# The covariance of a whitening kernel: one 128-column product per row, or one 64-column product for each sample group in its own half of TensorE

## The chip, the cores and the metric

The kernel runs on one core of a Trainium2 chip. The metric is the device time of one execution in microseconds (us); the numbers below are of a single program on a single core, so no other core waits for it.

## What is computed

The input `x` is 4 images of 64 channels, 256 by 256, in float32. There are two layers.

```
# layer 0: a long convolution of every channel with a separable filter hx * hy (zero-padded FFT of size 512)
y   = irfft2(rfft2(x) * rfft2(k) / fft_size)[..., :256, :256] + x * bias
# layer 1: whitening over channels, from every 9th position of every channel
x1   = transpose(y, (1, 0, 2, 3)).reshape(64, -1)
x1_s = x1[:, ::9]
cov  = x1_s @ x1_s.T / x1_s.shape[1] + 0.01 * eye(64)
deconv = newton_schulz_inverse_sqrt(cov, 5 iterations)
out  = deconv @ (x1 - mean(x1_s))
```

The kernel does the convolution as products with Toeplitz matrices, and the change touches only how `x1_s @ x1_s.T` and the sums for the mean are formed.

## The kernel before, in words

**Convolution.** 128 units (`UNITS`): two sweeps of 64 channels, two images (`PER`) in a unit. For each unit `q`, `make_v` and `make_y` each issue four groups of matmuls: three in the rounded type fp32r with 256 moving columns (lines 666 to 668) and one in float32 with 128 moving columns (line 669). A float32 matmul of the program is two LDWEIGHTS and two MATMUL instructions in the profile, so 58 of them are 116 instructions of each kind; an fp32r one is a single pair. ScalarE rounds `x` and `v` (L434, L443) and flips the filters (L424, L425), VectorE subtracts (L523, L532) and finishes `y` with the bias (`finish_y`, L543), GpSimd multiplies `y` by a 0/1 mask that keeps every ninth position (L400), and VectorE sums each group of nine columns into `z_sb` (`sum_masked`, L551): one of the nine is a sample, the others are zero.

**z_sb.** It has `ZROWS` = 58 rows `r`. A row holds, for each of the 128 partitions, 129 float32 columns (`ZW`): 64 channels of sample group j = 0, 64 channels of sample group j = 1, and one column of ones. A sweep fills it once.

**Covariance.** For each of the 58 rows one float32 matmul takes the 128 channel columns as stationary and all 129 as moving, and accumulates 128 x 129 results. Of these only the two diagonal 64 x 64 blocks and the column of sums are used; the two off-diagonal blocks mix group 0 with group 1 and are thrown away. It is done twice: for sweep 0 inside the unit loop at `q == C + 2` = 66, into PSUM bank 2, and copied to `sums_first` (L564); for sweep 1 after the loop, into bank 0, on top of `sums_first`, which a matmul with the identity puts there first (line 726). The two blocks are then copied to `sums`, the upper one by ScalarE (L463), the lower one by VectorE (L603, L604), and added by a matmul with `twice` (line 739).

**After it.** Five Newton-Schulz steps (lines 746 to 761) with `keep_busy` matmuls (L717) between them give `dmat`; then 64 tiles of 1 MB (`TILES`) are multiplied by it (line 777), shifted by the mean on ScalarE (L475) and VectorE (L646), and stored. The first sweep's and second sweep's `y` went to DRAM (`convolved`), so tiles are loaded again. 14 tiles (`KEPT`) are loaded during the second sweep, 12 more around its end (L314), each as its room in SBUF comes free: the last four of these wait for `cov_mm`, 2, since they land on `z_sb`. Then in the transform the loads follow the stores. All DMAs are issued by SyncE's queue in program order.

**What orders the work.** Every engine's order is written out by hand, and semaphores join them. TensorE runs `make_v(q + 1)`, `make_y(q)`, and at `q == 66` the covariance, then `make_y(66)`, `make_v(67)`. The covariance waits for `z_done`; VectorE waits for `cov_mm` before it copies and goes on.

Of the kernel before, what the change touches and what calls it, by code (L numbers as in the profile page):

```python
# [13 lines left out]
P = 128  # L14
B, C, S = 4, 64, 256
# [30 lines left out]
ZROWS = BLOCKS * GROUPS // 2  # L46
ZW = 2 * C + 1
# [19 lines left out]
def conv_whiten(nc, x, first, hidden, columns, bias, out):  # L67
# [3 lines left out]
    with ExitStack() as ctx:  # L71
        def sb(name, shape, dt=F32):
            return ctx.enter_context(nc.sbuf_tensor(name, shape, dt))
# [40 lines left out]
        z_sb = z_all[:, :].rearrange("p (r m) -> p r m", m=ZW)  # L114
# [3 lines left out]
        mask = sb("mask", [P, MASK_COLS])  # L118
        bias_sb = sb("bias_sb", [P, C])
        ident = sb("ident", [P, P])  # L120
        sums, sums_first = sb("sums", [P, C + 1]), sb("sums_first", [P, ZW])
        small = sb("small", [P, 8])
        col = sb("col", [P, 4])
        chan_i, chan, rate = sb("chan_i", [P, 1], I32), sb("chan", [P, 1]), sb("rate", [P, 1])
# [23 lines left out]
        for t in range(TILES):  # L148
# [3 lines left out]
            k = in_at[t]  # L152
# [14 lines left out]
        ps = ctx.enter_context(nc.psum_tensor("ps", [P, 8, S * 2], F32))  # L167
# [39 lines left out]
            return x_sb[slot].rearrange("p (b h w) -> p b h w", b=PER, h=HB)[:, :, h, :]  # L207

        def z_of(c):
            return z_sb[:, :, 0:2 * C].rearrange("p r (j c) -> p r j c", j=2)[:, :, :, c]  # L210

        def grouped(k, lo, hi):
            return masked[k][:, lo:hi, :].rearrange("p i w -> p (i w)").rearrange("p (r j u) -> p r j u", j=2, u=STRIDE)
# [136 lines left out]
        @block.gpsimd  # L350
        def _(pool):
            n_step = [0]

            def chained(ins):

                n_step[0] += 1
                ins.then_inc(pool_step, 1)
                pool.wait_ge(pool_step, n_step[0])

            def split_x(q):  # L360
                if q >= UNITS:
                    return
                k = q % 2

                wait(pool, x_hi_done, q + 1)
                nc.gpsimd.tensor_tensor(x_lo[k], row_block(q % X_SLOTS, 0), x_hi[k].bitcast(F32),  # L366
                                        ALU.subtract).then_inc(x_lo_done, 1)

            nc.gpsimd.memset(w_sb, 0.0).then_inc(w_zeroed, 1)
            nc.gpsimd.iota(pos_i, pattern=[[-1, S]], base=S - 1, channel_multiplier=0)  # L370
            chained(nc.gpsimd.iota(chan_i[:], pattern=[[0, 1]], base=0, channel_multiplier=1))
            nc.gpsimd.tensor_copy(pos, pos_i)
            nc.gpsimd.tensor_copy(chan[:], chan_i[:]).then_inc(pos_ready, 1)
            nc.gpsimd.memset(filt, 0.0).then_inc(filt_zeroed, 1)
            nc.gpsimd.memset(small[:], 0.0).then_inc(filt_zeroed, 1)
            nc.gpsimd.iota(index.bitcast(I32), pattern=[[1, MASK_COLS]], base=0,
                           channel_multiplier=S % STRIDE).then_inc(index_ready, 1)
            split_x(0)

            for k in range(2):  # L380
                nc.gpsimd.memset(masked[k][:, :, S:], 0.0)
            chained(nc.gpsimd.memset(ident[:], 0.0))
            chained(nc.gpsimd.affine_select(out=ident[:], in_=ident[:], compare_op=ALU.not_equal, fill=1.0,
                                            base=0, pattern=[[-1, P]], channel_multiplier=1))
            chained(nc.gpsimd.memset(z_sb[:, :, 2 * C:], 1.0))
            split_x(1)

            def mask_y(q):
                if q < 0:
                    return  # L390
                k = q % 2
                wait(pool, y_done, q + 1)

                wait(pool, z_done, q - 1)
                if q == LAST - 1:
                    for b in range(PER):
                        nc.gpsimd.tensor_tensor(masked_of(k, b, 1), by_image(y_sb[k])[:, b:b + 1],
                                                mask_of(SWEEPS - 1, b, 1), ALU.mult).then_inc(masked_half, 1)
                    return
                nc.gpsimd.tensor_tensor(masked_of(k, 0, PER), by_image(y_sb[k]), mask_of(q // C, 0, PER),  # L400
                                        ALU.mult).then_inc(masked_done, 1)

            for q in range(UNITS):
                split_x(q + 2)
                mask_y(q - 1)


            nc.gpsimd.tensor_scalar(ident15, ident[:], 1.5, None, ALU.mult)
            chained(nc.gpsimd.tensor_scalar(ident_eps, ident[:], EPS, None, ALU.mult))
            for k in range(2):  # L410
                nc.gpsimd.tensor_tensor(twice[:, k * C:(k + 1) * C], ident[:, 0:C], ident[:, C:P], ALU.add)
            pool.wait_ge(z_last_done, 2 * PER)
            nc.gpsimd.memset(halves, 0.5).then_inc(ident_ready, 1)

        @block.scalar
        def _(act):
            def flip(q):
                if q >= UNITS:
                    return
                k, h = q % T_SLOTS, q % H_SLOTS  # L420
                act.wait_ge(hankel_loaded[h], 32 * (q // H_SLOTS + 1))

                wait(act, y_mm, q - T_SLOTS + 1)
                nc.scalar.copy(t_f32[k], hankel[h][:, :, :P - 1:-1])  # L424
                nc.scalar.copy(t_hi[k], hankel[h][:, :, ::-1]).then_inc(flipped, 1)  # L425

            def round_x(q):
                if q >= UNITS:
                    return
                k = q % X_SLOTS  # L430
                act.wait_ge(x_loaded[k], 16 * (q // X_SLOTS + 1))

                wait(act, v_mm, q - 1)
                nc.scalar.copy(x_hi[q % 2], row_block(k, 0)).then_inc(x_hi_done, 1)  # L434

            def round_v(q):
                k = q % 2
                wait(act, v_mm, q + 1)

                wait(act, y_mm, q - 1)  # L440
                nc.scalar.copy(v_f32[k], ps_v[k][:, :, S:2 * S])  # L441

                nc.scalar.copy(v_hi[k], ps_v[k][:, :, 0:S]).then_inc(v_hi_done, 1)  # L443

            act.wait_ge(rate_ready, 1)
            nc.scalar.activation(decay, pos, ACT.Exp, scale=rate[:]).then_inc(decay_ready, 1)
            round_x(0)
            for layer in range(3):
                act.wait_ge(f_dve, layer + 1)
                nc.scalar.activation(hid, arg, ACT.Sin).then_inc(f_sin, 1)  # L450
            round_x(1)
            flip(0)
            flip(1)

            for q in range(UNITS):
                round_v(q)
                round_x(q + 2)
                flip(q + 2)

            act.wait_ge(filt_zeroed, 2)  # L460
            nc.scalar.activation(small[:, 7:8], small[:, 7:8], ACT.Sqrt)
            act.wait_ge(cov_mm, 2)
            nc.scalar.copy(sums[C:P, :], ps[C:P, 0, C:ZW]).then_inc(sums_upper, 1)  # L463
            act.wait_ge(norm_mm, 1)
            nc.scalar.activation(small[:, 1:2], ps[:, 0, 0:1], ACT.Sqrt).then_inc(n_act, 1)
            act.wait_ge(n_act, 1)
            nc.scalar.activation(small[:, 3:4], small[:, 1:2], ACT.Sqrt).then_inc(n_act, 1)
            act.wait_ge(d_ready, 1)

            for t in range(TILES):  # L470
                act.wait_ge(t_mm[0], t + 1)

                wait(act, t_stored[out_at[t]], 16 * stores_before_out[t])
                src = ps[:, bank(t, 0):bank(t, 0) + 2, :].rearrange("p r n -> p (r n)")
                nc.scalar.activation(places[out_at[t]][:, 0:TW // 2], src, ACT.Identity,  # L475
                                     bias=small[:, 6:7]).then_inc(t_act, 1)

        @block.vector
        def _(dve):
# [77 lines left out]
            for q in range(UNITS):  # L557
                split_v(q)
                finish_y(q - 1)
                split_t(q + 2)  # L560
                if q == C + 2:

                    dve.wait_ge(cov_mm, 1)
                    nc.vector.tensor_copy(sums_first[:], ps[:, 2, 0:ZW]).then_inc(cov_out, 1)  # L564
                if q < LAST:
                    sum_masked(q - 2)

# [32 lines left out]
            sum_half(LAST, 1)  # L600

            dve.wait_ge(cov_mm, 2)
            nc.vector.tensor_copy(sums[0:C, 0:C], ps[0:C, 0, 0:C])  # L603
            nc.vector.tensor_copy(sums[0:C, C:C + 1], ps[0:C, 0, 2 * C:ZW]).then_inc(sums_ready, 1)  # L604
            chained(nc.vector.memset(cov, 0.0))
            dve.wait_ge(ident_ready, 1)
            dve.wait_ge(cov_mm, 3)
# [42 lines left out]
        def _(pe):  # L650
# [44 lines left out]

            def covariance(bank_of_cov, rows, first):
                for r in rows:
                    last = mm(ps[:, bank_of_cov, 0:ZW], z_sb[:, r, 0:2 * C], z_sb[:, r, :],  # L698
                              start=(r == first), stop=(r == ZROWS - 1))
                return last  # L700

            make_v(0)
# [20 lines left out]


            pe.wait_ge(v_lo_done, LAST)
            mm(ps[:, 0, 0:ZW], ident[:], sums_first[:], start=True, stop=False)
            pe.wait_ge(z_done, LAST - 1)
            for b in range(PER):
                w = ZROWS // PER
# [81 lines left out]
```

## Time and profile before

| | before |
|---|---|
| time, median of 3 runs | 936.75 us (936.08 to 941.52) |
| time of the profiled execution | 937.11 us |
| its span in the trace | 934.9 us |
| granted TensorE clock, mean | 0.995 |
| PE busy | 865.4 us (93%) |
| PEld busy | 729.6 us (78%) |
| DVE busy | 577.7 us (62%) |
| POOL busy | 494.3 us (53%) |
| ACT busy | 401.6 us (43%) |
| DMA | 306.35 MB, mean 328 GB/s |

PE is TensorE's matmuls, PEld its weight loads, which run beside them. Spans are between the first and the last record of the trace; the time of an execution is a little longer (937.11 against 934.9 us). A matmul's duration in the trace is its latency; several are in flight at once, so what one costs in a row of them is the distance from start to start. Where a row has a count, its busy time is the union of their durations.

### The profile page before, as it was taken

The numbers are of one execution on the slowest core, as the hardware profiler recorded it, in microseconds if no ns is written. First come the engines' busy times: TensorE is split into PE (matmuls) and PEld (weight loads), VectorE is DVE, ScalarE is ACT, GpSimd is POOL, SyncE is SP. The second block draws the span as 40 slices with busy tenths as digits, with TensorE's granted clock in tenths as the row PEclk, the third lists the DMA queues.
The fourth block names the chain that finished last, engine by engine and source line by source line (L and its number), as shares of the span: only waits on it lengthen the run. The fifth ranks groups of instructions, "written<-read, shape, count | busy, mean of one in ns | idle before, by whom it ended". The sixth has DMA issues, their size and how long they took to land.

```text
span 934.9 us, 15604 instructions
## 1 busy us (share of the span) xinstructions
PE 865.4 (93%) x5970; PEld 729.6 (78%) x5970; DVE 577.7 (62%) x641; ACT 401.6 (43%) x715; POOL 494.3 (53%) x278
## 2 busy tenths in 40 slices
PE   2699999999999999999999999999999999977773
PEld 0699999999999999999999999999644444432221
DVE  5388888888878856787887787875333333322221
ACT  2355555555555534555555555551133333321220
POOL 2298888888888865787887778873000000000000
PEclk9999999999999999999999999999999999999997
DMA  3799999999989984999999999997999999999998
GB/s 106 242 305 287 282 284 285 283 281 287 288 278 296 285 256 150 348 342 321 358 345 314 323 331 353 344 325 256 407 381 422 423 424 422 426 427 427 427 427 342
DMA packets 99349, 306.35 MB, mean 328 GB/s; under 512 B 13483, under 2 KB 48332, under 8 KB 84684
## 3 DMA queue, kind: packets, MB, share of 16 engines
q1 hardware_dynamic: 99276, 305.37, 91.8%
q8 instruction: 47, 0.77, 0.3%
q14 instruction: 26, 0.21, 0.1%
HBM read 167.96 MB, written 137.36 MB: 327 GB/s over the span
## 4 chain that ended last, share of the span: by engine, by line
PE 83%; DMA 12%; DVE 2%; issue 1%; ACT 1%; SPq 0%; DVEq 0%
PE ps L669 24%; PE ps L777 15%; PE ps L666 13%; PE ps L667 13%; PE ps L668 13%; DMA arena<-convolved 11%; PE ps L698 3%; DVE arena L503 1%; PE ps L717 0%; DMA arena<-filters 0%; ACT arena L475 0%; DVE arena L646 0%; PE ps L657 0%; SPq L317 0%; DMA arena<-hidden 0%
## 5 line engine op out<-in xcount | busy, mean ns | idle before, releaser
L669 PE MATMUL ps<-arena 128*128 128x128 f32 x2048 | 393.8, 274 | 0.0
L666 PE MATMUL ps<-rounded 128*128 128x256 f32 x1024 | 373.7, 365 | 11.5 <-DVE rounded L532 8.7
L400 POOL TENSOR_TENSOR arena<-arena,mask 128x1024 f32<-128x1024 f32 x126 | 325.7, 2585 | 69.1 <-DVE arena L543 68.8
L669 PEld LDWEIGHTS ps<-arena 128*128 128x128 f32 x2048 | 315.9, 190 | 0.0
L668 PE MATMUL ps<-rounded 128*128 128x256 f32 x1024 | 288.8, 282 | 0.0
L667 PE MATMUL ps<-rounded 128*128 128x256 f32 x1024 | 288.2, 281 | 0.0
L777 PE MATMUL ps<-arena 128*128 128x512 f32 x488 | 215.7, 597 | 25.6 <-DMA arena<-convolved 25.6
L543 DVE SCALAR_TENSOR_TENSOR arena<-arena,bias_sb,ps 128x1024 f32<-128x1024 f32 x127 | 162.6, 1280 | 91.3 <-PE ps L669 45.8
L777 PEld LDWEIGHTS ps<-arena 128*128 128x128 f32 x488 | 90.8, 190 | 149.5 <-issue 105.7
L666 PEld LDWEIGHTS ps<-rounded 128*128 128x128 f32 x1024 | 196.8, 192 | 12.7 <-issue 12.7
L366 POOL TENSOR_TENSOR rounded<-arena,rounded 128x512 fp32r<-128x512 f32 x128 | 165.2, 1291 | 77.3 <-ACT rounded L434 76.6
L667 PEld LDWEIGHTS ps<-rounded 128*128 128x128 f32 x1024 | 197.3, 193 | 0.0
L668 PEld LDWEIGHTS ps<-rounded 128*128 128x128 f32 x1024 | 192.9, 188 | 0.0
L646 DVE TENSOR_SCALAR arena<-ps,small 128x1024 f32<-128x1024 f32 x64 | 82.2, 1284 | 170.3 <-PE ps L777 170.3
L551 DVE TENSOR_REDUCE arena<-arena 128x116 f32<-128x1044 f32 x126 | 155.5, 1234 | 0.0
L475 ACT ACTIVATE arena<-ps,small 128x1024 f32<-128x1024 f32 x64 | 71.2, 1113 | 188.5 <-PE ps L777 188.5
L441 ACT COPY arena<-ps 128x512 f32<-128x512 f32 x128 | 75.0, 586 | 171.2 <-PE ps L669 171.1
L523 DVE TENSOR_TENSOR rounded<-ps,rounded 128x512 fp32r<-128x512 f32 x128 | 88.1, 688 | 33.0 <-ACT rounded L443 32.6
L434 ACT CAST rounded<-arena 128x512 fp32r<-128x512 f32 x128 | 80.5, 629 | 45.7 <-DMA arena<-x 45.4
L532 DVE TENSOR_TENSOR rounded<-arena,rounded 128x512 fp32r<-128x512 f32 x128 | 89.7, 701 | 12.5 <-ACT rounded L425 12.4
L424 ACT COPY arena<-arena 128x256 f32<-128x256 f32 x128 | 51.8, 405 | 80.9 <-PE ps L669 67.6
L425 ACT CAST rounded<-arena 128x512 fp32r<-128x512 f32 x128 | 78.9, 617 | 0.0
(93 smaller groups left out, 218.9 us busy)
## 6 DMA issues: line engine op xcount, KB each, us to landing
arena<-x SPq DMA_DIRECT2D x128, 512.0 KB, 5.4
convolved<-arena SPq DMA_DIRECT2D x256, 256.0 KB, 5.3
out<-arena SPq DMA_DIRECT2D x64, 1024.0 KB, 11.8
arena<-convolved SPq DMA_DIRECT2D x47, 1024.0 KB, 17.6
arena<-filters SPq DMA_DIRECT2D x256, 128.0 KB, 4.7
arena<-convolved SPq DMA_DIRECT2D x28, 512.0 KB, 6.0
filters<-arena SPq DMA_DIRECT2D x16, 192.0 KB, 3.5
rounded<-convolved SPq DMA_DIRECT2D x3, 1024.0 KB, 8.8
```

Of the source, the lines that this page charges most:

```text
L366: nc.gpsimd.tensor_tensor(x_lo[k], row_block(q % X_SLOTS, 0), x_hi[k].bitcast(F32), ALU.subtract).then_inc(x_lo_done, 1)
L400: nc.gpsimd.tensor_tensor(masked_of(k, 0, PER), by_image(y_sb[k]), mask_of(q // C, 0, PER), ALU.mult).then_inc(masked_done, 1)
L523: nc.vector.tensor_tensor(v_lo[k], ps_v[k][:, :, 0:S], v_hi[k].bitcast(F32), ALU.subtract).then_inc(v_lo_done, 1)
L532: nc.vector.tensor_tensor(t_lo[k], hankel[h][:, :, ::-1], t_hi[k].bitcast(F32), ALU.subtract).then_inc(t_lo_done, 1)
L543: nc.vector.scalar_tensor_tensor(y_sb[k], x_sb[q % X_SLOTS], bias_sb[:, q % C:q % C + 1], ps_y[k].rearrange("p a n -> p (a n)"), ALU.mult, ...
L551: nc.vector.tensor_reduce(z_of(q % C), grouped(q % 2, 0, BLOCKS), AX_X, ALU.add).then_inc(z_done, 1)
L646: nc.vector.tensor_scalar(places[out_at[t]][:, TW // 2:TW], src, small[:, 6:7], None, ALU.add).then_inc(t_dve, 1)
L666: mm(wide, hi[:, b, cols], t_hi[k][:, f, :], start=True, stop=False)
L667: mm(wide, hi[:, b, cols], t_lo[k][:, f, :], start=False, stop=False)
L668: mm(wide, lo[:, b, cols], t_hi[k][:, f, :], start=False, stop=False)
L669: last = mm(o[:, b, m * S + P:(m + 1) * S], block1[:, b, cols], t_f32[k][:, f, :], start=False, stop=True)
L777: last = mm(ps[:, bank(t, u) + r, :], dmat, places[k][:, w:w + IMG], start=True, stop=True)
```

## The change

The two groups' products are made apart. A row of `z_sb` is laid out anew: group 0, the ones, group 1. For each row there are two matmuls in place of one: group k has 64 stationary columns and 65 moving ones (its channels and the ones), writes 64 PSUM partitions, and has the tile position `(0, 64 * k)`, that is all 128 rows of the array and one half of its columns. For group 1 the ones come first, so its sums stand in column 0 of its half, and the copies to `sums` follow: ScalarE now makes two, VectorE one.

```diff
-        sums, sums_first = sb("sums", [P, C + 1]), sb("sums_first", [P, ZW])
+        sums, sums_first = sb("sums", [P, C + 1]), sb("sums_first", [P, C + 1])
...
         def z_of(c):
-            return z_sb[:, :, 0:2 * C].rearrange("p r (j c) -> p r j c", j=2)[:, :, :, c]
+
+            return z_sb[:, :, c:c + C + 2:C + 1]
...
-            chained(nc.gpsimd.memset(z_sb[:, :, 2 * C:], 1.0))
+            chained(nc.gpsimd.memset(z_sb[:, :, C:C + 1], 1.0))
...
             act.wait_ge(cov_mm, 2)
-            nc.scalar.copy(sums[C:P, :], ps[C:P, 0, C:ZW]).then_inc(sums_upper, 1)
+            nc.scalar.copy(sums[C:P, C:C + 1], ps[C:P, 0, 0:1])
+            nc.scalar.copy(sums[C:P, 0:C], ps[C:P, 0, 1:C + 1]).then_inc(sums_upper, 1)
...
                     dve.wait_ge(cov_mm, 1)
-                    nc.vector.tensor_copy(sums_first[:], ps[:, 2, 0:ZW]).then_inc(cov_out, 1)
+                    nc.vector.tensor_copy(sums_first[:], ps[:, 2, 0:C + 1]).then_inc(cov_out, 1)
...
             dve.wait_ge(cov_mm, 2)
-            nc.vector.tensor_copy(sums[0:C, 0:C], ps[0:C, 0, 0:C])
-            nc.vector.tensor_copy(sums[0:C, C:C + 1], ps[0:C, 0, 2 * C:ZW]).then_inc(sums_ready, 1)
+            nc.vector.tensor_copy(sums[0:C, :], ps[0:C, 0, 0:C + 1]).then_inc(sums_ready, 1)
...
             def covariance(bank_of_cov, rows, first):
                 for r in rows:
-                    last = mm(ps[:, bank_of_cov, 0:ZW], z_sb[:, r, 0:2 * C], z_sb[:, r, :],
-                              start=(r == first), stop=(r == ZROWS - 1))
+
+                    for k in range(2):
+                        lo = k * (C + 1)
+                        last = mm(ps[k * C:(k + 1) * C, bank_of_cov, 0:C + 1], z_sb[:, r, lo:lo + C],
+                                  z_sb[:, r, k * C:(k + 1) * C + 1], start=(r == first), stop=(r == ZROWS - 1),
+                                  tile_position=(0, k * C))
                 return last
...
-            mm(ps[:, 0, 0:ZW], ident[:], sums_first[:], start=True, stop=False)
+            mm(ps[:, 0, 0:C + 1], ident[:], sums_first[:], start=True, stop=False)
```

**Where the instructions stand.** On TensorE between `make_y(65)` and `make_y(66)`, before the change (the size is partitions of the output by its columns, the stationary width being the first):

```order
L666 MATMUL ps<-rounded 128x256
L667 MATMUL ps<-rounded 128x256
L668 MATMUL ps<-rounded 128x256
L669 MATMUL ps<-arena 128x128
L698 MATMUL ps<-arena 128x129 x58
L666 MATMUL ps<-rounded 128x256
```

At the same place with the change, where line 698 has become 702 and 666 to 669 have become 667 to 670:

```order
L667 MATMUL ps<-rounded 128x256
L668 MATMUL ps<-rounded 128x256
L669 MATMUL ps<-rounded 128x256
L670 MATMUL ps<-arena 128x128
L702 MATMUL ps<-arena 64x65 x116
L667 MATMUL ps<-rounded 128x256
```

Nothing moved; 58 matmuls of the program became 116 of half the width. On TensorE at the end of the unit loop, before the change, from the busy-keeping matmuls to the norm of the covariance:

```order
L717 MATMUL ps<-ident 128x128 x9
L726 MATMUL ps<-sums_first,ident 128x129
L698 MATMUL ps<-arena 128x129 x58
L717 MATMUL ps<-ident 128x128 x3
L739 MATMUL ps<-sums,arena 128x65
L717 MATMUL ps<-ident 128x128 x5
L742 MATMUL ps<-small,arena 128x1
```

And with it:

```order
L722 MATMUL ps<-ident 128x128 x9
L731 MATMUL ps<-sums_first,ident 128x65
L702 MATMUL ps<-arena 64x65 x116
L722 MATMUL ps<-ident 128x128 x3
L744 MATMUL ps<-sums,arena 128x65
L722 MATMUL ps<-ident 128x128 x5
L747 MATMUL ps<-small,arena 128x1
```

Here too the order stays, and the matmul with the identity has 65 moving columns in place of 129.

## Rows read from the trace of the kernel before

**Rows 1.** The page: TensorE's clock and the DMA in 40 slices of the span

```profile
PE   2699999999999999999999999999999999977773
...
PEclk9999999999999999999999999999999999999997
DMA  3799999999989984999999999997999999999998
GB/s 106 242 305 287 282 284 285 283 281 287 288 278 296 285 256 150 348 342 321 358 345 314 323 331 353 344 325 256 407 381 422 423 424 422 426 427 427 427 427 342
```

**Rows 2.** Stretches: PE, PEld, DVE, ACT, POOL busy (and count), clock, DMA share, GB/s

```profile
200.00:300.00 100.00, 100.00 (x870) 100.00 (x869) 80.47 (x87) 55.29 (x110) 87.67 (x44) 1.00 0.91 286
340.00:354.00 14.00, 14.00 (x127) 14.00 (x126) 2.41 (x5) 0.93 (x2) 3.56 (x2) 1.00 0.52 168
400.00:500.00 100.00, 100.00 (x865) 100.00 (x864) 78.02 (x86) 54.75 (x109) 78.42 (x44) 1.00 0.99 339
```

**Rows 3.** Chain that ended last, in order of time: start, us, what

```profile
340.51 12.96 PE ps L698 x116
...
644.01 13.19 PE ps L698 x116
657.21 0.67 PE ps L717 x6
...
669.16 134.02 PE ps L777 x312
803.21 1.29 DVE arena L646
804.57 0.33 SPq L317
804.95 23.49 DMA arena<-convolved
```

**Rows 4.** Timeline, around the second covariance's start

```profile
643.98 0.19 PEld L698 LDWEIGHTS ps<-arena 128*128 128x128 f32 x1 [1.28 <-issue]
644.01 0.35 PE L698 MATMUL ps<-arena 128*128 128x129 f32 x1 [1.11 <-DVE arena L581]
```

**Rows 5.** Timeline from 657.80 to 657.90 us: 65 moving columns

```profile
657.60 0.28 PE L717 MATMUL ps<-ident 128*128 128x128 f32 x1
657.71 0.33 PE L739 MATMUL ps<-sums,arena 128*128 128x65 f32 x2
657.72 0.19 PEld L739 LDWEIGHTS ps<-sums,arena 128*128 128x128 f32 x1
657.83 0.19 PEld L717 LDWEIGHTS ps<-ident 128*128 128x128 f32 x1
657.88 0.33 PE L717 MATMUL ps<-ident 128*128 128x128 f32 x1
```

**Rows 6.** Tile `sums`: duration in ns, least/median/most

```profile
L739 PE MATMUL ps<-sums,arena x2: 222/248/275, 657.7 to 657.8; 128*128 128x65 f32 x2
L463 ACT COPY sums<-ps x1: 209/209/209, 657.2 to 657.2; 64x65 f32<-64x65 f32 x1
L604 DVE COPY sums<-ps x1: 141/141/141, 657.4 to 657.4; 64x1 f32<-64x1 f32 x1
```

**Rows 7.** Timeline after the first covariance, in `make_y(66)`

```profile
353.77 0.19 PEld L666 LDWEIGHTS ps<-rounded 128*128 128x128 f32 x1
353.80 0.36 PE L666 MATMUL ps<-rounded 128*128 128x256 f32 x1
```

**Rows 8.** Stretches after the unit loop, columns as in rows 2

```profile
644.00:654.00 10.00, 9.99 (x89) 10.00 (x90) 2.42 (x4) 0.00 (x0) 0.31 (x2) 1.00 1.01 405
654.00:658.00 4.00, 4.00 (x38) 4.00 (x37) 0.42 (x3) 0.21 (x1) 0.00 (x0) 1.00 0.97 315
658.00:676.00 18.00, 17.20 (x88) 11.64 (x88) 7.38 (x26) 2.60 (x4) 0.00 (x0) 1.00 1.02 425
...
676.00:688.00 12.00, 12.00 (x30) 5.30 (x29) 5.14 (x4) 3.34 (x3) 0.00 (x0) 1.00 0.93 339
...
800.00:928.00 128.00, 94.87 (x208) 37.32 (x206) 34.44 (x27) 28.95 (x26) 0.00 (x0) 0.99 1.01 427
```

**Rows 9.** Who waited for whom: total us, times, longest

```profile
PE ps L777 <- DMA arena<-convolved: 25.6, 22, 1.2
```

**Rows 10.** SyncE's queue: the first stores of the transform

```profile
674.17 7.13 SPq L317 DMA_DIRECT2D out<-arena  x3
```

## The prediction

> **What bounds the kernel now.** I read the page's slices first [rows 1]: TensorE is busy in all but the first and the last ten slices, at full clock, and the DMA is near its ceiling (427 GB/s) only in those last ones. So there are two stages. In the unit loop TensorE has no gap over 100 us at a time [rows 2], VectorE and GpSimd are at 80 to 88%, and the DMA at 286 GB/s: time taken off TensorE there comes off the end. In the second stage, the transform of 64 tiles, the stretches show the DMA at 1.01 and 427 GB/s from 800 us on while TensorE is at 95 of 128 us [rows 8], and TensorE waits for loads 22 times, 25.6 us in all [rows 9]: there the bytes set the end. Between them lies the second covariance.
>
> The chain has the two covariances as pieces of 12.96 and 13.19 us, each of 116 MATMUL instructions [rows 3]. The first is wholly TensorE's: in its 14 us VectorE, ScalarE and GpSimd come nearly to rest and the DMA falls to 168 GB/s [rows 2]. During the second the DMA moves 405 GB/s [rows 8]: tiles are loaded beside it.
>
> **The covariance itself.** 58 rows in 13.1 us are 0.226 us a row, two pairs of a load and a matmul of 0.113 us each. What limits a pair? The last small matmul before the norm tells. It has 128 stationary columns and 65 moving ones. Its first instruction starts at 657.71; the two together are busy 0.33 us and the second lasts 275 ns [rows 5, 6], so the second starts at 657.71 + 0.33 - 0.275 = 657.77, 0.06 us later: 65 moving columns cost 59 ns or so, half of what 129 cost. But the loads stand at 657.60, 657.72 and 657.83 [rows 5], 0.11 us apart although the columns stream in half the time: a load of 128 columns takes 0.11 us by itself. So before the change load and stream are equal, and both are halved by it: 59 ns for the stream, and, as an estimate by columns, 56 ns for the load of 64. But there are four pairs a row in place of two. One after the other they make 4 x 59 = 236 ns, a little more than the 226 of before. **All of the gain hangs on whether the two halves of the array work at the same time.**
>
> If they do, the order in the program still limits them: half 0's two instructions come one after the other (59 ns), then half 1's first may start beside half 0's second, then 59 ns, then the next row. A row is 2 x (59 + d), where d is the step from one half to the other. No row shows such a step. The nearest is a switch between types of matmul: the second instruction of line 669 starts about when the load of L666 does, at 353.77, and the matmul of L666 at 353.80 [rows 7], so 0.03 us. So d is between 0 and 28 ns with overlap (and 59 without). I take the middle, 14: a row is 146 ns, a covariance 58 x 0.146 = 8.5 us in place of 13.1, **4.6 us less**. With d = 0 it is 118 ns a row and 6.3 us less, with d = 28 it is 174 ns and 3.0 us less.
>
> Entering and leaving the divided array may need the pipeline empty, twice per covariance. No row shows it; it is bounded by nothing and by one latency of 275 ns each time [rows 6]. I take the whole, 0.5 us for a covariance, since I don't see what would hide it.
>
> The page "TensorEngine Tiling (Array Packing)" of the Trainium skill, section Key Properties, says that different tiles can load and multiply in parallel and that a change of tiling mode drains TensorE; no row here shows either. Another page of the Trainium skill, "TensorE: Matmul & The Clock Gate", section "Back-to-back issue gap", gives about 81 ns per pair of load and matmul at 128 moving columns as the sustained rate; by it four pairs would be 324 ns a row, 5.7 us more in each covariance. It was not measured in float32, and the 59 ns in this trace between two matmuls with 65 columns are below it.
>
> **First covariance.** TensorE is alone on the path, so 4.6 - 0.5 = 4.1 us come off in full. What is behind it is ready: the x slots are full, since the DMA has come down to 168 GB/s beside it [rows 2], and VectorE's copy to `sums_first` has 65 columns rather than 129 and is beside `make_y(66)`. `z_of` writes two groups 65 columns apart rather than 64: the same 116 sums per unit, no cost, hidden by TensorE anyway (VectorE is at 80% [rows 2]).
>
> **Second covariance.** It also ends 4.1 us sooner, and so do `dmat` and the first store. The small edits: ScalarE copies twice; the second one adds about 0.14 us (as L604's 141 ns for a single column [rows 6]), VectorE saves as much, and the `keep_busy` instructions after the covariance (0.67 us [rows 3]) cover both copies. Nothing. What the 4.1 us are worth depends on the DMA, which is the bound soon after. Its rate when full is 425 GB/s [rows 8]. From 654 to 658 it moves 315: 4 x (1 - 315/425) = 1.0 us of transfer lost. I read that as the early loads running out before the four tiles that land on `z_sb` may go (they wait for this covariance). From 676 to 688 it moves 339: 12 x (1 - 339/425) = 2.4 us lost, the 12 first tiles being in and the stores only starting. An earlier covariance fills such holes and nothing else. By bytes they are 3.5 us; by the share of time in which DMA engines rest, 4 x 0.03 + 12 x 0.07 = 1.0 us, the rest being slow packets that would stay slow. The gain here is between 1.0 and 3.5; I take **2.0 us**, nearer to the lower end, since in the stretches of 315 GB/s the share is 0.97. So about half of the second covariance's gain is given back.
>
> **Sum.** 4.1 + 2.0 = 6.1 us. The profiled execution took 937.11 us, so 931.0 by it; it lies 0.36 us over the median of 936.75, and against that the forecast is 930.7. Ends of this case: 6.3 - 0 + 3.5 = 9.8, 927.0; 3.0 - 0.5 + 1.0 = 3.5, 933.3.
>
> **Rivals.**
>
> *No overlap (also: the tile position changes nothing).* The halves take turns, or their loads do. 4 x 59 = 236 ns a row, 58 x 0.010 = 0.6 us more, and 0.5 for the mode: 1.1 us more in each. In the second one the later `dmat` starves the DMA for as long, so 2.2 in all: 938.9; with loads at 56 ns as the limit and no drain it is 936.5. For it: in this trace a load never overlaps another load of the same kind closer than 0.11 us, though durations of 0.19 us overlap, so there is one load path now. Against: nothing, but nothing in the trace speaks for a second path being closed either.
>
> *The load is no longer hidden (slower).* Before, each load runs beside the matmul in front of it. When the array has to be waited for, a matmul starts 31 ns after its load at the earliest: 643.98 and 644.01 [rows 4], 353.77 and 353.80 [rows 7]. If in a divided array every pair shows that much of its load, and the halves don't overlap, a pair is 59 + 31 = 90 ns, a row 360 ns and a covariance 20.9 us, 7.8 more; twice, and 0.5 each for the mode, is 16.6: 953. If the whole load of 56 ns shows, a row is 460 ns and it is 26.7 us, 13.6 more, twice with the mode 28.2: 965. It is slower by over 1% from about 4.7 us per covariance on, 81 ns a row less the 10 of the turns, so from 18 ns shown of each load. It speaks for it that each half is loaded anew while it is in use; against it, that in rows of before the load of the next matmul starts while the last one is in flight, in the same rows and columns of the array [rows 5]. The Trainium skill, "TensorE: Matmul & The Clock Gate", section "The mechanism", names a rule that would bring it about: loads overlap with matmuls in flight only when their row group differs (or when they go to the background buffer), and both halves here use all rows. By the rule's first half alone the load would not have been hidden before either, and the trace shows it hidden.
>
> *The clock.* Each matmul now uses half of the array. The granted clock is 1.00 through both covariances [rows 2, 8] with a full one. If it fell to the lower level in them, pitches would double: from 8.5 us to 17, some 4 us above before in each, 943 to 946. I see no row that speaks for it.
>
> **How the numbers follow.** A measurement of this kernel can tell about 1% (9.4 us) from no change: faster is under 927.4, slower over 946.1. Overlap 0.52 (927 to 933), no overlap 0.27 (936 to 939), load shown 0.16 (up to 945 for small parts of it, 0.03; 953 to 965, 0.13), clock 0.05. The likeliest is overlap, at 930.7. Faster by over 1% needs nearly both best ends at once: 0.07. Slower by over 1%: 0.13 from shown loads and 0.02 from the clock, 0.15. The rest, 0.78, is within. The range of 8 in 10 begins at the best end of the overlap, 927, takes in the turns and small shown loads, and ends at 944; 965 is left out.
>
> **What would show it.** In the changed trace the covariance's group has 464 matmul instructions; the piece of the chain should be 6.8 to 10.1 us long rather than 13. Loads of the two halves at nearly the same start, and matmuls of 64x65 alternately 59 and about 14 ns apart, show overlap; an even 56 to 59 ns shows turns; 90 or more shows the load. The stretch from 340 us on should end 4 us sooner, the first store (674.17 before [rows 10]) by 8 us, the last transfer by only 6, and the hole of 315 GB/s should be smaller. If the first covariance is 4 us shorter and the end moves by 4 alone, the second one's share was mis-sized; if it moves by 8, the DMA was not the bound that I take it for.

## The result, and the profile after

The changed kernel took a median of 930.75 us (926.39 to 934.42, 8 runs) against 939.57 us (936.08 to 941.52, 8 runs) for the kernel before, measured together: ratio 0.9901, 95% interval 0.9877 to 0.9926. That is 9.3 us less (7.0 to 11.6). The forecast was 6.1 us less than 936.75, the median of the three runs shown before; the absolute numbers nearly meet, 930.7 and 930.75, but that is luck: the kernel before came out 2.8 us slower in the larger set. The saving was half as large again as forecast, and the forecast saving lies just outside the measured interval.

The chain of the changed kernel, in order of time (start, us, what), answers to [rows 3]; the span is 927.3 us (934.9 before):

```profile
339.34 6.92 PE ps L702 x232
...
638.13 6.60 PE ps L702 x219
644.74 1.35 issue
646.08 0.57 PE ps L702 x13
646.66 0.86 PE ps L722 x6
...
658.78 127.16 PE ps L782 x296
785.96 1.29 DVE arena L647
787.32 0.33 SPq L318
787.70 23.33 DMA arena<-convolved
```

The first covariance is 6.92 us in place of 12.96, with twice as many instructions. The second is 6.60 + 1.35 + 0.57 = 8.52 us in place of 13.19, with a pause of 1.35 us near its end that the first does not have.

The group of the covariance's instructions, durations in ns (least, median, most), and the timeline around 340.25 us and at the end of the first covariance:

```profile
L702 PEld LDWEIGHTS ps<-arena x464: 132/138/138, 339.3 to 646.4; 128*64 128x64 f32 x155
L702 PE MATMUL ps<-arena x464: 218/222/271, 339.3 to 646.4; 128*64 128x65 f32 x155
```

```profile
340.08 0.46 PE L702 MATMUL ps<-arena 128*64 128x65 f32 x10
...
345.79 0.46 PE L702 MATMUL ps<-arena 128*64 128x65 f32 x10
345.91 0.20 PEld L702 LDWEIGHTS ps<-arena 128*64 128x64 f32 x4
346.18 0.19 PEld L667 LDWEIGHTS ps<-rounded 128*128 128x128 f32 x1
```

Ten matmuls of 0.222 us fill 0.46 us, so the last starts 0.46 - 0.22 = 0.24 us after the first: nine steps of 0.027 us on average, where each alone was to cost 0.059. In the single records the starts of the matmuls come in pairs, 7 ns apart, with a pair every 58 ns, and those of the loads do the same: the two halves run side by side. At the end the last matmul starts at 346.03 (345.79 + 0.46 - 0.22) and the next load at 346.18; that is 0.15 us, some 0.09 more than a step of 0.058.

The stretches, columns as in [rows 2] and [rows 8]:

```profile
340.00:354.00 14.00, 14.00 (x283) 13.93 (x278) 4.52 (x6) 3.26 (x8) 3.62 (x3) 1.00 0.45 136
...
640.00:658.00 18.00, 15.86 (x250) 14.16 (x246) 6.53 (x27) 0.64 (x4) 0.20 (x1) 1.00 1.00 403
658.00:690.00 32.00, 32.00 (x79) 14.41 (x78) 10.94 (x11) 10.03 (x9) 0.00 (x0) 1.00 1.00 395
690.00:800.00 110.00, 109.90 (x256) 48.18 (x254) 40.89 (x32) 35.65 (x32) 0.00 (x0) 1.00 1.01 427
800.00:920.00 120.00, 85.13 (x185) 33.06 (x184) 30.81 (x24) 25.62 (x23) 0.00 (x0) 0.98 1.01 427
```

The clock stays at its full level in both covariances. The first store is issued at 663.79 in place of 674.17 [rows 10], 10.4 us earlier, and the span ends 7.6 us earlier: 2.8 us were given back in the DMA-bound stage. Single spans are to be read with care here: short pauses of TensorE in the second sweep, which the profile gives as "issue" and which come and go from run to run (none in e1_first_only, 7.2 us in sum in e5_second_left_out), move the start of the second covariance by several microseconds whatever the kernel.

### The profile page after: what moved, and what is told of

Same layout as the page of the kernel before. It is cut to its first block, busy times and chain, and to the rows that moved or that the text cites. A ratio compares the mean times of both kernels' runs of the same rounds, so it can differ in the third digit from the quotient of the medians.

```text
span 927.3 us, 16068 instructions
## 1 busy us (share of the span) xinstructions
PE 854.4 (92%) x6202; PEld 717.6 (77%) x6202; DVE 578.9 (62%) x640; ACT 400.7 (43%) x716; POOL 494.4 (53%) x278
## 4 chain that ended last, share of the span: by engine, by line
PE 73%; DMA 17%; DVE 3%; SPq 3%; issue 1%; ACT 1%; DVEq 0%; ACTq 0%
PE ps L670 21%; PE ps L782 15%; PE ps L667 12%; PE ps L668 11%; PE ps L669 11%; DMA arena<-convolved 11%; DMA convolved<-arena 4%; PE ps L702 2%; DMA arena<-x 1%; SPq L262 1%; DVE arena L545 1%; SPq L272 1%; SPq L318 1%; DVE arena L505 1%; PE ps L722 0%
## 5 line engine op out<-in xcount | busy, mean ns | idle before, releaser
L534 DVE TENSOR_TENSOR rounded<-arena,rounded 128x512 fp32r<-128x512 f32 x128 | 91.8, 717 | 11.5 <-ACT rounded L426 11.5
```

The lines of the kernel that those rows point to most:

```text
L534: nc.vector.tensor_tensor(t_lo[k], hankel[h][:, :, ::-1], t_hi[k].bitcast(F32), ALU.subtract).then_inc(t_lo_done, 1)
```

## The experiments

The profiled lengths of the first covariance are compared first (from the chain), then the times. Runs with one time only are read for their traces.

**e3_half_by_half, e4_two_rows, e7_blocks_16, e11_blocks_4: does the order of the halves matter?** The edit is the same in all, with `BLOCK` 58, 2, 16 and 4 (the changed kernel has 1):

```diff
-                for r in rows:
-                    for k in range(2):
+                rows = list(rows)
+                for at in range(0, len(rows), BLOCK):
+                    for k in range(2):
+                        for r in rows[at:at + BLOCK]:
```

> The kernel after, with the same matmuls in another order: in each call of covariance all of half 0's rows, then all of half 1's. Theory A (a matmul starts only after the one before it in the program has, so two halves work together only where they alternate): 232 instructions at 58 ns, 13.5 us for the first covariance, as before the change. Rival B (the gain is from smaller loads and streams and not from working at the same time): the order doesn't matter, 6.9 us.

> As the kernel after, but two rows of half 0, then two rows of half 1, in turn. If matmuls start strictly in the program's order, with a step of nearly nothing from one half to the other, two rows take 2 x (4 - 1) x 58 = 348 ns, a row 174 ns and the first covariance 10.1 us. If TensorE starts a matmul of the free half ahead of one that waits for the busy half, it is 6.9 us again. If the order of the two float32 passes in the machine isn't that of the program (the starts 7 and 51 ns apart in the changed kernel could mean that), it is something between.

> As the order with two rows, but 16 rows of half 0, then 16 rows of half 1 (32 instructions of each kind in a run). Two rows gave full overlap and 58 rows none. If TensorE looks ahead in a window of 64 instructions, loads counted, it sees the other half only in the last part of each run: about half of the overlap, a first covariance of 9 to 12 us. If the window is much smaller it is about 12.5 to 13.5 us, if larger 7.2.

> Four rows of half 0, then four rows of half 1 (runs of 8 matmul instructions). With 16 rows the starts came in pairs for about three instructions around each switch from one half to the other, and the first covariance took 12.5 us: (32 - 3) x 7.25 x 0.058. By the same look-ahead of three instructions, four rows give (8 - 3) x 29 x 0.058 = 8.4 us. If the look-ahead is longer than that it is 7.2 us, as with two rows.

The pieces of the chain of e3_half_by_half, e7_blocks_16 and e11_blocks_4, in this order:

```profile
340.27 13.50 PE ps L703 x232
```

```profile
339.66 12.43 PE ps L703 x232
```

```profile
339.46 8.66 PE ps L703 x229
```

The group of e4_two_rows, in the window of the first covariance:

```profile
L703 PE MATMUL ps<-arena x232: 219/222/271, 339.2 to 346.2; 128*64 128x65 f32 x116
```

In e4_two_rows the first covariance is 7.18 us from the first record to the last (6.99 in the changed kernel, 13.57 in e3_half_by_half, 12.50 in e7_blocks_16, 8.73 in e11_blocks_4). So half by half each step is 13.50 / 232 = 0.058 us, and the whole gain is gone with the same instructions, the same loads and the same streams: **it comes from the two halves working at the same time**, and rival B is out. Theory A, as it was put before the run, is out too: with two rows in a run, strict order of starts would have made 10.1 us, and it was 7.2. TensorE starts matmuls of one half while earlier ones of the other half still wait, but only a few ahead. In the single records of e7_blocks_16 the starts are 58 ns apart within a run, and for about three steps at each change of half they come in pairs. From a look-ahead of three, 8.4 us was expected for four rows in a run, and it was 8.7.

**e8_narrow: what sets the 58 ns?**

```diff
-                    covariance(2, range(ZROWS), 0).then_inc(cov_mm, 1)
+                    covariance(2, range(1), 0)
+                    covariance(2, range(1, ZROWS), 0, 33).then_inc(cov_mm, 1)
```

(The last argument is the number of moving columns. The sums that the missing columns would give are left out, and `covariance` got the argument for it; the lines of that are not shown.)

> The kernel after, but in the first covariance rows 1 to 57 have 33 moving columns in place of 65 (the rest of the sums of sweep 0 is left out); the stationary 64 stay. If the load of 64 columns sets the pitch as well as the stream (56 against 59 ns), the first covariance stays at about 6.6 us. If the load is hidden entirely, it falls to about 3.5 to 4 us.

```profile
341.74 6.89 PE ps L702 x232
```

6.89 us with 33 moving columns and 6.92 with 65: with half of the moving columns a step is no shorter, so the stream is not what holds it at 58 ns. I read it as the load: 64 float32 columns in 58 ns, where 128 take 0.11 us [rows 5]. No run changed the stationary width alone, so a fixed cost of a float32 pair is not ruled out. Halving the moving columns alone would have brought nothing. Both halves load every 58 ns, so their loads, too, run side by side.

**e9_switches: what does it cost to divide and join the array?**

```diff
                                   tile_position=(0, k * C))
+                    if bank_of_cov == 2:
+                        mm(ps[:, 3, 0:1], ident[:], ident[:, 0:1], start=True, stop=True)
```

> The kernel after, but in the first covariance each row's two halves are followed by one float32 matmul of the whole array (128 stationary columns, 1 moving) into a bank that nothing reads: the array is divided and joined 58 times in place of once. The extra matmul's two loads of 128 columns take 2 x 0.11 us, so without a cost of the switch a row is 0.117 + 0.22 = 0.34 us and the first covariance 19.7 us. If each switch empties the pipeline and costs up to one latency of 0.275 us, twice a row, it is up to 0.89 us a row, 52 us. By what the changed trace shows at the end of the covariance (0.15 us from the last matmul's start to the next load) I expect 0.1 us for each switch, 31 us.

The first covariance took 50.65 us, where 31 was expected. Pieces of the chain near its start and near its end, and stretches of it:

```profile
343.71 0.27 PE ps L702 x4
343.97 0.31 PE ps L706 x2
...
390.11 0.41 PE ps L702 x4
390.52 0.52 PE ps L706 x2
```

```profile
344.00:347.00 3.00, 3.00 (x32) 2.58 (x32) 0.00 (x0) 0.00 (x0) 1.27 (x1) 1.00 0.96 282
...
345.00:390.00 45.00, 45.00 (x300) 38.42 (x296) 0.00 (x0) 0.00 (x0) 0.27 (x1) 0.52 0.07 26
```

At full clock a row of six matmuls takes 0.27 + 0.31 = 0.58 us. Without a cost of the switch it would be 0.34, so two switches cost 0.24 us, 0.12 each, close to the 0.1 expected. From 345 to 390 us the granted clock is 0.52, that is the lower level for nearly all of it, and a row takes 0.41 + 0.52 = 0.93 us. Ten rows at 0.58 and 48 at 0.93 make 50 us; all 58 at full clock would be 34. TensorE was never idle by the profile in those 45 us, so the time at the switches is counted as busy there. The changed kernel makes this switch four times in all, which by this price is 0.5 us.

**e1_first_only and e2_second_only: what is each covariance worth?** Both use the layout of before, with a column of ones ahead of row 0, so that group 0 can take the ones of the row ahead; `covariance_halves` is used in one place, the old function in the other (the copies to `sums` and `sums_first` that go with it are not shown).

```diff
+            def covariance_halves(bank_of_cov, rows, first):
+                for r in rows:
+                    for k in range(2):
+                        at = 1 + r * ZW + k * C
+                        last = mm(ps[k * C:(k + 1) * C, bank_of_cov, 0:C + 1], z_all[:, at:at + C],
+                                  z_all[:, at - 1 + k:at + C + k], start=(r == first), stop=(r == ZROWS - 1),
+                                  tile_position=(0, k * C))
+                return last
```

> Only the covariance of sweep 0 (at unit 66) is made by halves; that of sweep 1 keeps the 128-column matmuls of before. To serve both, group 0's ones are read from the column ahead of its row, and VectorE makes three small copies to sums_first. My theory (the first covariance lies on TensorE's path alone, its 6.0 us come off in full): time 6.0 us below before, ratio 0.9936, the first covariance's piece 6.9 us, the second's about 13 us. Rival (what the end gained came from the second one, which released DMAs earlier, and the first one's gain is taken back in the second sweep, where the DMA share is 0.99): less than 2 us below before.

> The mirror: only the covariance of sweep 1, after the unit loop, is made by halves. My theory (the DMA sets the end of the second stage, so an earlier second covariance only fills holes in it): first store 6 us earlier than in before against the end of the unit loop, but the time only 1 to 3 us below before, 2.0 by the prediction's value, ratio 0.998. Rival (the path goes through the covariance and the norm to the end): 6 us below before, ratio 0.9935.

e1_first_only: 935.24 us (12 runs) against 940.59 (23 runs), ratio 0.9942 (0.9918 to 0.9966), 5.5 us less (3.2 to 7.7). Its first covariance took 7.1 us in place of 13.0; these 5.8 us are inside, and the rival's less than 2 us is out. e2_second_only: 937.33 us (12 runs), ratio 0.9955 (0.9926 to 0.9984), 4.2 us less (1.5 to 7.0; the two medians differ by 3.3). The interval holds both the 2.0 of the prediction and the rival's 6; it doesn't decide.

**e5_second_left_out and e12_later_norm: the same question from both sides.** The first leaves out 56 of the 58 rows of the second covariance.

```diff
-                last = covariance(0, range(b * w, (b + 1) * w), -1)
+                last = covariance(0, range((b + 1) * w - 1, (b + 1) * w), -1)
```

> The kernel after, but the covariance of sweep 1 leaves out 56 of its 58 rows (only row 28 and row 57 go in), so the whitening rests on too few samples; everything else is done. The second covariance falls from 6.9 us, 8.5 with its pause, to about 0.3. If the DMA sets the end of the second stage, little is left to gain from it: 0 to 2 us below the kernel after, 0.990 to 0.988 against before. If the covariance is on the path to the end, 6 to 8 us below the kernel after: ratio 0.982 to 0.983.

```diff
-            keep_busy(3)
+            keep_busy(33)
```

> The kernel after, with 33 in place of 3 busy-keeping matmuls between the second covariance and the addition of its halves: 60 instructions of 0.111 us, 6.7 us. The four loads that wait for the second covariance go as early as in the kernel after, but the matrix dmat and the first store come 6.7 us later, as if that covariance were as long as before. If what an earlier second covariance brings comes by way of the first store (holes in the DMA's work after the first loads are in), the time is 2 to 4 us above the kernel after: ratio 0.992 to 0.9945 against before. If it comes by the release of the four loads, or if nothing of it reaches the end, it is that of the kernel after, 0.990; if TensorE's chain sets the end, 6.7 us more: 0.997.

e5_second_left_out: 931.59 us (6 runs), ratio 0.9921 (0.9890 to 0.9951). It is no faster than the changed kernel (0.9901); by the two intervals at most 2 us of gain can hide. The covariance did not shrink to the 0.3 us expected, though. Around it, by the chain:

```profile
646.77 1.22 DVE arena L583 x2
647.99 0.04 issue
648.04 0.48 PE ps L702 x4
648.52 1.58 PE ps L722 x6
```

Its second part waits for the samples that VectorE sums last (L583), so from its first matmul to the end of its last it takes 3.0 us in place of 8.5. And TensorE, idle for 1.67 and 2.16 us before the two parts, then runs at the lower clock for a while, so that the steps to `dmat` take longer:

```profile
648.00:653.00 5.00, 4.96 (x25) 4.85 (x26) 1.54 (x7) 0.35 (x3) 0.20 (x1) 0.50 1.02 421
```

The transform starts 3.9 us earlier than in the changed kernel (the table below), not 8. e12_later_norm: 937.88 us (12 runs), ratio 0.9971 (0.9943 to 0.9998), so 0.0070 above the changed kernel, 6.6 us, with an uncertainty of some 3.5 from the two intervals: delaying `dmat` costs it all or most of 6.7 us, though the four loads go as early. It was above the range of 2 to 4 that my theory gave, and at the rival's value; the traces below put it at 6.6. The hole that the theory asked for is there, though it is not the whole of it. From 658 to 690 us, e12_later_norm:

```profile
658.00:690.00 32.00, 31.84 (x90) 15.45 (x91) 11.41 (x15) 8.92 (x8) 0.00 (x0) 1.00 0.92 365
```

The DMA engines rest for 8% and move 365 GB/s, where the changed kernel has 1.00 and 395.

Since the pauses of the second sweep blur the times, I also took from each trace the length of the second stage alone, which is the time from the first matmul of the second covariance to the end of the span, beside the time from the same matmul to the transform's first one:

| kernel | to the transform, us | to the end, us |
|---|---|---|
| e12_later_norm | 27.4 | 295.8 |
| e3_half_by_half | 26.8 | 295.5 |
| before | 25.0 | 290.9 |
| e1_first_only | 25.0 | 292.1 |
| e7_blocks_16 | 24.5 | 293.4 |
| e11_blocks_4 | 21.4 | 288.3 |
| e2_second_only | 20.9 | 291.8 |
| changed | 20.5 | 289.2 |
| e4_two_rows | 20.5 | 289.1 |
| e8_narrow | 20.4 | 288.4 |
| e9_switches | 20.3 | 287.4 |
| e5_second_left_out | 16.6 | 288.4 |
| e10_bf16_whole | 16.2 | 288.7 |
| e6_bf16 | 15.6 | 290.6 |

The mean of the three around 25 us is 292.1, of the six around 21 us 289.0, of the three around 16 us 289.2; single values scatter by 1 to 2 us, so a difference of two means is uncertain by about 1 us. Going from 25 to 21 us brought 3.1 us at the end, and going on to 16 us nothing: there the DMA sets the end. Above 21 us the end moves with the transform's start. (The transform's start in e3_half_by_half and e5_second_left_out contains a stretch at the lower clock.)

Where do these microseconds lie? The first 270 us of that stage, before, changed and e12_later_norm:

```profile
644.01:914.01 270.00, 244.81 (x695) 116.02 (x696) 88.53 (x94) 69.73 (x66) 0.30 (x2) 1.00 1.01 419
```

```profile
638.13:908.13 270.00, 241.06 (x814) 110.24 (x814) 88.59 (x94) 70.83 (x67) 0.20 (x1) 1.00 1.01 421
```

```profile
634.25:904.25 270.00, 242.35 (x863) 115.13 (x864) 87.14 (x92) 68.71 (x66) 0.30 (x2) 1.00 1.00 415
```

The stage moves about 120 MB in all three. Against 427 GB/s these stretches have lost 5.1, 3.8 and 7.6 us of transfer. So of the 6.6 us by which e12_later_norm is longer than the changed kernel, 3.8 are such holes. The other 2.8 lie in the last 19 to 26 us of the span, where the last stores land, and no run shows why. The means of the groups in these 270 us are 418, 420.5 and 421 GB/s, so holes account for about half of the 3.1 us.

**e6_bf16 and e10_bf16_whole: a version that is faster than both.** The samples are rounded to bfloat16 as VectorE writes them; the rest is as in the changed kernel (e6_bf16) or as in the kernel before (e10_bf16_whole).

```diff
-        z_sb = z_all[:, :].rearrange("p (r m) -> p r m", m=ZW)
+        z_sb = z_all[:, :].bitcast(mybir.dt.bfloat16)[:, 0:ZROWS * ZW].rearrange("p (r m) -> p r m", m=ZW)
```

> The kernel after with the samples z_sb in bfloat16, so each matmul is one pair of instructions and not two, and the samples are rounded (64 stationary, 65 moving columns, still by halves). If the load of 64 columns sets the pitch (0.056 us by columns from the 0.11 us of 128), both covariances take 58 x 0.056 = 3.3 us in place of 6.9; if the stream does, which is one pass of 65 columns, 58 x 0.03 = 1.7 us. Time against the kernel after: 3.6 to 5.2 us less from the first, and a third to two thirds of it from the second: 5 to 8 us less, ratio against before 0.982 to 0.985. Rival (the second stage's DMA takes all back, or VectorE's writes of two bytes are slower and hold up the unit loop): ratio 0.990 or more.

> The kernel before, undivided, with the samples in bfloat16 (rounded): 58 pairs of 128 stationary and 129 moving columns, one pass. If bfloat16 alone does what it did by halves (2.06 us), the halves no longer matter: 2 us and ratio 0.986. If a load of 128 columns takes twice that of 64 (0.030 us by halves), a pair is about 0.06 us, the first covariance 3.5 us, and the ratio 0.988 to 0.990.

The first covariance, e6_bf16:

```profile
340.40 1.99 PE ps L703 x116
```

and e10_bf16_whole:

```profile
341.58 3.44 PE ps L699 x58
```

By halves a row is 1.99 / 58 = 0.034 us and undivided 3.44 / 58 = 0.059. e6_bf16 took 927.12 us (4 runs) against 939.24, ratio 0.9864 (0.9845 to 0.9884); e10_bf16_whole 928.96 us (6 runs) against 940.38, ratio 0.9871 (0.9826 to 0.9915). Both beat the kernel before; the first is also 0.0037, 3.5 us, below the changed kernel (0.9901), with an uncertainty of some 3 us from the two intervals. The expectation for e6_bf16 (0.982 to 0.985) asked for a further gain from the second covariance, which the table has shown isn't there (and its second part waited 1.4 us for VectorE's last samples). The first alone is 6.92 - 1.99 = 4.9 us shorter, which makes 0.985, and that is within the interval. In bfloat16 the halves save 1.5 us once, which these intervals can't show. The prices are a rounding of the samples and a covariance that is less exact.

## Why the prediction was right, and where it was off

The mechanism held: the two halves work at the same time, the first covariance counts in full and the second in part. The size of the saving was too small, by the step d above all.

- *What bounds the kernel* held. The first covariance was worth what it was shortened by (5.8 us by the trace of e1_first_only, 5.5 by the times), the second only a part, with the DMA's floor right behind it (the table, e5_second_left_out).
- *The pitch of 59 ns* for 65 columns, from the one matmul with 65 moving columns [rows 5, 6], held: 58 ns. The load of 64 columns, an estimate of 56 ns by columns, fits too: no more than 58, and e8_narrow shows that the stream is not what holds the step there.
- *"The order in the program still limits them"* is the step that failed. The forecast added a step d of 14 ns from half to half, for a row of 146 ns and 4.6 us saved. The changed kernel needs 6.92 / 58 = 0.119 us a row, twice 59 ns with nothing added. That alone would also fit the program's order with d = 0; e4_two_rows decides, since it took 7.2 us and not the 10.1 of that order. With the order not binding, d drops out: 6.0 us saved and not 4.6, close to the best end of 6.3. The row taken for d [rows 7], a matmul 28 ns after another one, is a switch of type and says nothing of halves.
- *The switch of mode*, 0.5 us per covariance, was too much: 0.12 us each way (e9_switches), 0.24 per covariance, and already inside the 6.92 us.
- *First covariance:* 4.1 us forecast, 6.0 by the trace, 5.5 (3.2 to 7.7) by e1_first_only. This is the larger part of the miss.
- *Second covariance:* it was to get 4.1 us shorter and bring 2.0. It got 4.7 us shorter, its pause included, and brought 3.1 by the table, 4.2 (1.5 to 7.0) by e2_second_only. The term was of the right kind, and somewhat small; only half of the 3.1 us are the holes that it was reasoned from. That the earlier covariance also moves the first loads, as the forecast had it, isn't shown apart. e12_later_norm, which leaves them early, ends no sooner than e3_half_by_half, where they go late and the transform starts about as late (295.8 and 295.5 us), so they seem to matter little.
- *Sum:* 6.0 + 3.1 = 9.1 us by the traces, 9.3 (7.0 to 11.6) by the times; the forecast's best end was 9.8. Faster by over 1% had a chance of 0.07 and the measured ratio is on that edge; with d left open between 0 and 28 that chance was too small.
- *No overlap* and *the load is no longer hidden* are out: half by half, where the halves can't overlap, still costs 58 ns a step, so the load stays hidden even then. Nor did the four pairs of a row take 324 ns: it was 119. The rule of the Trainium skill, "TensorE: Matmul & The Clock Gate", section "The mechanism", that loads overlap with matmuls in flight only when their row groups differ, would have left the load unhidden in these halves, which share all rows, and it was hidden; whether the page's exception, the background weight buffer, is what hides it, no run here shows. The page "TensorEngine Tiling (Array Packing)" of the Trainium skill, section Key Properties, fits in both points: tiles load and multiply in parallel (a pair of loads and a pair of matmuls every 58 ns), and a change of mode costs time (0.12 us in e9_switches; that it is a drain, no run shows).
- *The clock* did not fall in the changed kernel. That it can was shown elsewhere (e9_switches).

## What to carry to other kernels

A product whose off-diagonal blocks are thrown away was made here by halves of TensorE's columns at half the cost, loads and streams alike. That held as long as the halves alternated in the program every few matmuls; in long runs of one half the gain was gone. Divide the array once for a whole batch, not per matmul. Before shortening work at the border of two stages, ask how much of the next stage's resource is idle: here the first four microseconds brought about three and the next five nothing that can be seen.

## What was not expected

- TensorE takes matmuls of the free half ahead of the program's order, by about three: the first covariance took 7.2 us with runs of 4 instructions per half, 8.7 with 8, 12.5 with 32, 13.6 with 116.
- With an array that is divided and joined at each row, the granted clock went to the lower level (1.00 in the stretch to 347 us, 0.52 from 345 to 390), with no idle time in the records of TensorE.
- A pause of TensorE stands in the second covariance of seven kernels: 1.1 to 1.7 us in the changed kernel, e2_second_only, e4_two_rows, e8_narrow, e9_switches and e12_later_norm, 0.4 in e11_blocks_4. In five of them it is before the same instruction, the 220th of 232 (not in e2_second_only and e9_switches). In all seven the restart comes 1.4 to 1.6 us after a block of 16 KB of instructions has landed by DMA. Where TensorE goes through its instructions at little more than half that pace or slower (before, e1_first_only, e3_half_by_half, e7_blocks_16, e10_bf16_whole), there is none. It looks like TensorE outrunning its instruction supply while the DMA is full, but no run tested that, and it stays open.
